# Attention in a fused ViT block: transposed probabilities and values kept whole in float32, row maxima written negated

## The reference, cut to what matters

```
h = embed(x) ; prepend cls_tok                      # [16, 37, 192]
n = layernorm(h)
Q, K = rope(n @ Wq.T), rope(n @ Wk.T) ; V = n @ Wv.T   # 12 heads of 16
s = Q K^T / sqrt(16), causal mask, softmax over keys
h = h + (softmax(s) V) @ Wo.T
h = h + moe(layernorm(h))                           # 8 experts, top 2, hidden 768, exact gelu
```

## Time and profile before

| | |
|---|---|
| median of 3 runs | 245.99 us (243.65 to 252.13) |
| the profiled execution | 244.32 us, of which the span of the trace is 242.5 us |
| VectorE busy | 153.4 us, 63% |
| TensorE busy | 182.8 us, 75% |
| GpSimd busy | 96.1 us, 40% |
| mean granted TensorE clock | 0.802 of 2.4 GHz |

### The profile page before, as it was taken

The page is one execution under the profiler, slowest core; times in us unless marked ns, Lnnn a source line. Parts: engine busy times, 40 slices in busy tenths (PEclk is TensorE's granted clock), DMA queues, the critical chain, the costliest instruction groups (busy, mean ns, idle before and its releaser), DMA issues.

```text
span 242.5 us, 3838 instructions
## 1 busy us (share of the span) xinstructions
PE 182.8 (75%) x1065; PEld 140.7 (58%) x1065; DVE 153.4 (63%) x436; ACT 104.4 (43%) x313; POOL 96.1 (40%) x77
## 2 busy tenths in 40 slices
PE   3999999659799499729829343454899999999830
PEld 2887343245666295615815122254799999999720
DVE  0133756859878968797994888996356455564410
ACT  2011333477687366527030022900656566566500
POOL 1012265739404600853925736930023233433241
PEclk9999999977587956955555555559999999999995
DMA  6945999999999400100100795202032342422211
GB/s 164 312 111 138 278 285 279 285 279 251 201 194 210 112 3 1 39 0 4 39 0 13 213 278 143 50 26 76 22 63 38 59 59 42 67 52 20 33 19 16
DMA packets 25656, 27.12 MB, mean 112 GB/s; under 512 B 4880, under 2 KB 21928, under 8 KB 25634
## 3 DMA queue, kind: packets, MB, share of 16 engines
q1 hardware_dynamic: 21378, 24.16, 40.1%
q0 software_dynamic: 4256, 2.69, 7.8%
HBM read 23.73 MB, written 8.64 MB: 133 GB/s over the span
## 4 chain that ended last, share of the span: by engine, by line
PE 50%; DVE 23%; DMA 10%; issue 8%; ACT 3%; SPq 2%; POOL 1%; ACTq 0%; POOLq 0%; DVEq 0%
PE bank L708 8%; DMA out_y<-y,tokblk 7%; PE bank L463 6%; PE bank L534 5%; PE bank L732 4%; PE bank L489 4%; DVE sneg L1091 3%; DVE ao L1118 3%; PE bank L718 3%; DVE tablei L1240 3%; PE bank L495 2%; PE bank L734 2%; PE bank L550 2%; DVE pay L1015 2%; DMA wtok_sb<-in_w_tok 1%
## 5 line engine op out<-in xcount | busy, mean ns | idle before, releaser
L446 POOL DMA_INDIRECT out_y<-y,tokblk x14 | 21.9, 1562 | 55.2 <-DVE y L1281 23.8
L372 POOL TENSOR_TENSOR rstd<-veps,nhalf 111x1 f32<-111x1 f32 (+1 forms) x12 | 7.0, 584 | 58.5 <-DVE veps L999 58.5
L732 PE MATMUL bank<-we,hthi 128*128 x84 | 25.9, 371 | 1.4 <-DVE htlo L1272 1.4
L827 ACT ACTIVATE probs<-bank,sneg 111x111 f32<-111x111 f32 (+1 forms) x72 | 18.2, 347 | 18.2 <-DVE sneg L1091 18.1
L380 POOL TENSOR_TENSOR we<-raw,we 128x1152 fp32r<-128x1152 f32 x8 | 20.9, 2617 | 4.8 <-ACT we L883 4.7
L1091 DVE TENSOR_SCALAR sneg<-smax 111x4 f32<-111x4 f32 (+1 forms) x18 | 21.0, 1166 | 0.6
L708 PE MATMUL bank<-we,xahi 128*128 x56 | 20.2, 361 | 1.4 <-DVE xb L1254 1.4
L405 POOL DMA_INDIRECT dispatched<-pay,rowu x12 | 16.5, 1373 | 11.9 <-DVE rowu L1167 10.1
L734 PE MATMUL bank<-we,htlo 128*128 x84 | 21.1, 251 | 0.0
L463 PE MATMUL bank<-wtok_sb,x_sb 128*111 128x192 f32 (+1 forms) x72 | 17.5, 403 | 4.1 <-DMA wtok_sb<-in_w_tok 4.1
L947 ACT ACTIVATE hid<-bank 128x384 f32<-128x384 f32 x28 | 13.8, 492 | 10.2 <-PE bank L708 10.2
(11 more groups left out here) (162 smaller groups left out, 491.2 us busy)
## 6 DMA issues: line engine op xcount, KB each, us to landing
dispatched<-in_pad_rows SPq DMA_DIRECT2D x1, 5350.5 KB, 37.4
raw<-in_w SPq DMA_DIRECT2D x8, 576.0 KB, 12.8
raw<-in_w_a SPq DMA_DIRECT2D x8, 384.0 KB, 8.9
raw<-in_w_bb SPq DMA_DIRECT2D x8, 384.0 KB, 9.4
xin<-dispatched SPq DMA_DIRECT2D x14, 130.5 KB, 2.1
x_sb<-in_patches SPq DMA_DIRECT2D x5, 333.0 KB, 5.8
raw<-in_w_b SPq DMA_DIRECT2D x8, 192.0 KB, 9.1
wtok_sb<-in_w_tok SPq DMA_DIRECT2D x3, 192.0 KB, 3.5
```

Of the source, the lines that this page charges most:

```text
L446: pool.indirect_dma_start(out, bass.IndirectOffsetOnAxis(ap=tokblk[:, b:b + 1], axis=0), y[:, b % 2, :], None, compute_op=ALU.add).then_in ...
L732: mm(o[:, 0:2 * D], hthi[:, f, :], w, start=(f == 0), stop=False)
L827: last = fn(probs[0:n, b, hd, 0:n], bank[g][0:n, TOK * j:TOK * j + n], ACT.Exp, bias=sneg[0:n, b, hd:hd + 1], scale=float(HD) ** -0.5)
```

## The change

The transposed probabilities are copied whole to `pt` in float32: groups 0 and 1 by ScalarE (`turned`, where `high` was), group 2 by VectorE (where `low` of group 2 was). `low` and `high` of the second part go. `vp` is float32 with 17 columns a head (16 values and the one), written by one copy on ScalarE, so lines 797, 1061 and 418 go with their semaphores. `values` makes one float32 matmul a head. The scale 1/4 of the scores is put into the rope tables (each of cosine and sine is multiplied by 1/2), and the reduction for the row maxima writes the negated maximum at once, so that line 1091 goes. `norm_out` is a reciprocal and one multiplication that reads PSUM.

```diff
-PC = 2 * HD + 1
+PC = HD + 1
-        vp = early("vp", [TOK, TILES, HEADS, VC], BF16)
+        vp = early("vp", [TOK, TILES, HEADS, PC])
-        pth = second("pth", [TOK, 2, HEADS, TOK], FP16)
-        ptl = second("ptl", [TOK, 2, HEADS, TOK], FP16)
+        pt = second("pt", [TOK, 2, HEADS, TOK])
+        def turned_copied(engine, t, g):
+            if g < 2:
+                engine.wait_ge(pt_act, 2 * t + g + 1)
+            else:
+                engine.wait_ge(pt_dve, t + 1)
@@ gpsimd, after each tile's sum of line 415
-                pool.wait_ge(v2_ready, t + 1)
-                nc.gpsimd.tensor_tensor(vp[0:n, t, :, PC:VC], vr..., vp[0:n, t, :, HD + 1:PC], ALU.subtract)
@@ tensor, probs_t
-                        pe.wait_ge(ptl_ready, i - 1)
+                        turned_copied(pe, *divmod(i - 2, GROUPS))
@@ tensor, values
-                        pe.wait_ge(ptl_ready, GROUPS * t + hd // HG + 1)
+                        turned_copied(pe, t, hd // HG)
-                    mm(... pth, vp[0:PC]) ; mm(... pth, vp[PC:VC]) ; mm(... ptl, vp[0:PC])
+                    last = mm(bank[7][0:n, c:c + PC], pt[0:n, b, hd, 0:n], vp[0:n, t, hd, :], start=True, stop=True)
@@ scalar, v_parts
-                fn(vp[0:n, t, :, HD + 1:PC], vr[0:n, b, :]..., ACT.Copy).then_inc(v2_ready, 1)
@@ scalar, exps
-                              bias=sneg[0:n, b, hd:hd + 1], scale=float(HD) ** -0.5)
+                              bias=sneg[0:n, b, hd:hd + 1])
@@ scalar, the loop
-                    high(i - 1, 0) ; high(i - 1, 1)
+                    turned(i - 1, 0) ; turned(i - 1, 1)
...
-                    high(i - 1, 2)
@@ vector, rope
-                v.tensor_tensor(vr..., bank[2 + b]..., vp[0:n, t, :, 0:HD], ALU.subtract).then_inc(vr_ready, 1)
@@ vector, scores_max
-                    step(v.tensor_reduce(smax[0:n, b, hs], s, AX.X, ALU.max))
-                    v.tensor_scalar(sneg[0:n, b, hs], smax[0:n, b, hs], -float(HD) ** -0.5, None, ALU.mult)
+                    v.tensor_reduce(sneg[0:n, b, hs], s, AX.X, ALU.max, negate=True).then_inc(max_ready, 1)
@@ vector, in place of low
+            def turned(t, g):
+                dve.wait_ge(pt_done, i + 1)
+                if t >= 2:
+                    dve.wait_ge(pv_done, t - 1)
+                v.tensor_copy(pt[0:n, b, HG * g:HG * g + HG, 0:n], bank[3 + i % 2]...).then_inc(pt_dve, 1)
@@ vector, norm_out
-                v.reciprocal(rsum[0:n, b, :], o[:, :, HD])
-                step(v.tensor_copy(a, o[:, :, 0:HD]))
-                step(v.tensor_tensor(a, o[:, :, HD + 1:PC], a, ALU.add))
-                v.tensor_tensor(a, a, rsum..., ALU.mult)
+                step(v.reciprocal(rsum[0:n, b, :], o[:, :, HD]))
+                v.tensor_tensor(a, o[:, :, 0:HD], rsum..., ALU.mult)
@@ vector, the loop
-                    low(i - 1, (0, 1))
...
-                    low(i - 1, (2,))
+                    turned(i - 1, 2)
@@ tables on the host
-        "rope_cos": np.cos(m_theta).astype(np.float32)[pos],
+        "rope_cos": np.cos(m_theta).astype(np.float32)[pos] * np.float32(HD ** -0.25),
```

More of the change, by code:

```diff
@@ L58 @@
 EARLY = 6
-VC = 3 * HD + 1
 G0, G1, LG, CT = 0, TOK, 2 * TOK, 256
-PC = 2 * HD + 1
+PC = HD + 1
 BLOCK_WARM_UP = 18
@@ L236, in vit_block @@
         qk_ready = sem("qk_ready")
-        v1_ready = sem("v1_ready")
-        vr_ready = sem("vr_ready")
-        v2_ready = sem("v2_ready")
-        v3_ready = sem("v3_ready")
+        v_ready = sem("v_ready")
         ones_ready = sem("ones_ready")
@@ L248, in vit_block @@
         pt_done = sem("pt_done")
-        pth_ready = sem("pth_ready")
-        ptl_ready = sem("ptl_ready")
+        pt_act = sem("pt_act")
+        pt_dve = sem("pt_dve")
         pv_done = sem("pv_done")
@@ L491, in project @@
                 if t >= 2:
-                    pe.wait_ge(vr_ready, t - 1)
-                    pe.wait_ge(v1_ready, t - 1)
+                    pe.wait_ge(v_ready, t - 1)
                 for j, (a, w) in enumerate(((hnta, wqkva_sb), (hntb, wqkvb_sb))):
@@ L528, in scores @@
                     elif g == 2:
-                        pe.wait_ge(vr_ready, TILES - 1)
-                        pe.wait_ge(v1_ready, TILES - 1)
+                        pe.wait_ge(v_ready, TILES - 1)
                     q, k = (qta[:, b, 0:n], kbda[:, b, HG * g:HG * g + HG, 0:n]) if g < 2 else \
@@ L556, in values @@
                 n, b = ROWS[t], t % 2
-                pe.wait_ge(v3_ready, t + 1)
+                pe.wait_ge(v_ready, t + 1)
                 if t == 0:
@@ L564, in values @@
                     if hd % HG == 0:
-                        pe.wait_ge(ptl_ready, GROUPS * t + hd // HG + 1)
+                        turned_copied(pe, t, hd // HG)
                     c = hd * PC
-                    mm(bank[7][0:n, c:c + PC], pth[0:n, b, hd, 0:n], vp[0:n, t, hd, 0:PC], start=True, stop=False)
-                    mm(bank[7][0:n, c:c + HD], pth[0:n, b, hd, 0:n], vp[0:n, t, hd, PC:VC], start=False, stop=False)
-                    last = mm(bank[7][0:n, c:c + PC], ptl[0:n, b, hd, 0:n], vp[0:n, t, hd, 0:PC],
-                              start=False, stop=True)
+                    last = mm(bank[7][0:n, c:c + PC], pt[0:n, b, hd, 0:n], vp[0:n, t, hd, :], start=True, stop=True)
                 if hd == HEADS - 1:
@@ L837, in high @@
                     act.wait_ge(pv_done, t - 1)
-                fn(pth[0:n, b, HG * g:HG * g + HG, 0:n],
+                fn(pt[0:n, b, HG * g:HG * g + HG, 0:n],
                    bank[3 + i % 2][0:n, 0:HG * TOK].rearrange("p (h s) -> p h s", s=TOK)[:, :, 0:n], ACT.Copy)\
-                    .then_inc(pth_ready, 1)
+                    .then_inc(pt_act, 1)
             def copy_attended(t):
@@ L888, in _ @@
                 if i >= 1:
-                    high(i - 1, 0)
-                    high(i - 1, 1)
+                    turned(i - 1, 0)
+                    turned(i - 1, 1)
                 if i >= 2:
@@ L1089, in scores_max, with turned @@
                     s = bank[g][0:n, 0:HG * TOK].rearrange("p (h s) -> p h s", s=TOK)[:, :, 0:n]
-                    step(v.tensor_reduce(smax[0:n, b, hs], s, AX.X, ALU.max))
-                    v.tensor_scalar(sneg[0:n, b, hs], smax[0:n, b, hs], -float(HD) ** -0.5, None, ALU.mult)\
-                        .then_inc(max_ready, 1)
-            def low(t, groups):
+                    v.tensor_reduce(sneg[0:n, b, hs], s, AX.X, ALU.max, negate=True).then_inc(max_ready, 1)
+            def turned(t, g):
                 n, b = ROWS[t], t % 2
-                for g in groups:
-                    i = GROUPS * t + g
-                    hs = slice(HG * g, HG * g + HG)
-                    dve.wait_ge(pth_ready, i + 1)
-                    if t >= 2:
-                        dve.wait_ge(pv_done, t - 1)
-                    v.tensor_tensor(ptl[0:n, b, hs, 0:n],
-                                    bank[3 + i % 2][0:n, 0:HG * TOK].rearrange("p (h s) -> p h s", s=TOK)[:, :, 0:n],
-                                    pth[0:n, b, hs, 0:n], ALU.subtract).then_inc(ptl_ready, 1)
+                i = GROUPS * t + g
+                dve.wait_ge(pt_done, i + 1)
+                if t >= 2:
+                    dve.wait_ge(pv_done, t - 1)
+                v.tensor_copy(pt[0:n, b, HG * g:HG * g + HG, 0:n],
+                              bank[3 + i % 2][0:n, 0:HG * TOK].rearrange("p (h s) -> p h s", s=TOK)[:, :, 0:n])\
+                    .then_inc(pt_dve, 1)
             def norm_out(t):
@@ L1314, in constants @@
         "tok_sel": np.stack([tok % SEQ != 0, tok % SEQ == 0]).astype(np.float32),
-        "rope_cos": np.cos(m_theta).astype(np.float32)[pos],
-        "rope_sin": (np.sin(m_theta).astype(np.float32)[pos] * sign).astype(np.float32),
+        "rope_cos": np.cos(m_theta).astype(np.float32)[pos] * np.float32(HD ** -0.25),
+        "rope_sin": (np.sin(m_theta).astype(np.float32)[pos] * sign).astype(np.float32) * np.float32(HD ** -0.25),
         "mask": np.where(allowed, 0.0, -1e30).astype(bf16),
```

26 lines of the change are left out of this document (3 added, 23 removed).

## The result

The changed kernel takes 231.01 us (median of 4 runs, 229.52 to 231.54) where the kernel before takes 244.82 (4 runs beside it, 243.4 to 252.13): a ratio of 0.940, with 0.934 to 0.946 as its interval. The forecast was 232.0. The profiled execution's span is 229.3 us against 242.5. The ratios leave out runs in which a kernel was over 1.5% above its own fastest; the medians take in every run, so a difference of medians can be larger than the ratio beside it says.

What follows compares the result with a forecast made beforehand. The attention loop was taken to be bound by VectorE's SBUF instructions waiting behind GpSimd. A 12.3 us lead at tile 5's norm_out plus 0.6 in the tail gave 12.9, so 232 us; own range 228 to 235, overall 225.5 to 240.

Steps and rivals of the forecast that it cites:

- Opening: Up to the first maximum: tile 1's keys spread at about 43.9 instead of 44.86, 1.0 us gained; negated reduction nearly free.
- Tile 0: Loop's first norm_out: at about 56.5 us, ahead by 7.2, with 0.6 taken back by ScalarE and 1.0 by the values.
- Values on TensorE: Float32 matmuls in attention: pairs 0.20 or 0.37 us apart, 2.4 or 4.4 us a tile, losing 0.5 or 1.1.
- Steps 1 to 3: Loop: about 1 us net in steps 2 and 3, step 3's hold stays; tile 2's norm_out about 79, 9 ahead.
- Step 4: Loop: hold moves to choose until 96.7; tile 3's norm_out, about 92, isn't held; ahead by 10.
- Step 5: Loop: the 6.98 us stall is covered, choose then waits 1.4 us; 2 us more gained.
- Tail: After the last norm_out's start: two instructions fewer, 0.6 us; the stall at 135.77 stays, later distances kept.
- Rival 1: Loop: stalls only move from step 3 on, gain is the opening's 7.2 + 0.6: 236.5 us; chance 0.17.
- Rival 5: Row maxima: negation takes a second pass from SBUF that GpSimd holds, most stalls stay: 243 us; chance 0.07.
- Rival 3: Scatters wait for the padding copy landing at 83.75, capping Rival 2's gain at 13.5 + 3: 228 us; chance 0.03.
- Rival 4: Values: float32 weights aren't loaded beside the matmul before, so the kernel is slower: 263 us; chance 0.04.
- Rival 2: Steps 4 and 5: TensorE gets the higher clock, 5.4 us more gained: 226.5 us; chance 0.12.

Runs made afterwards that it cites:

- experiments 3 and 4: GpSimd's subtractions in the loop left out, low parts of weights filled by DMA: 3 from the kernel before, 227.94 us; 4 from the kernel after, 222.5 us.
- experiment 1: Kernel before with only the negated maxima (reduction writes them, line 1091 goes) and the scaled tables: 241.63 us, ratio 0.990.
- experiment 2: Kernel after with the negation given back as a second instruction from SBUF: 241.51 us, ratio 0.985.
- experiment 11: Kernel before with the negated reduction and norm_out's one product from PSUM, second part of the values left out of the sum: 236.96 us, ratio 0.964.
- experiment 5: Kernel after with norm_out copying to SBUF first and multiplying there: 237.54 us, ratio 0.960.
- experiment 6: Kernel after with two VectorE subtractions reading PSUM given back at the head of each step, into a scrap tile: 236.48 us.
- experiment 10: Kernel after with norm_apply's two instructions moved behind the step's last maximum, warm-up still 18: 236.39 us.
- warm_24: Kernel after with 24 instead of 18 warm-up matmuls before the first block: 227.12 us; again, beside the kernel after on one chip, 229.79 against 230.04.
- the two reorderings: Kernel after with GpSimd's subtractions ahead of router and scatters, 233.53 us; and with norm_apply behind the last maximum, 236.39 us.

## Why the prediction was right, step by step

**What bounds the loop.** Right, and shown: GpSimd's subtractions account for 11.0 of the loop's 13.9 us (experiments 3 and 4), the holds move in part to the next SBUF instruction when one is taken away (experiment 1), and 12.2 us come back when one is put back (experiment 2). The reductions and products with PSUM input ran beside GpSimd unhindered: 553 and 356 ns means. One bound was too low: I put the longest wait at the three subtractions' 6.2 us, though the earlier trace rows have one of 6.98. That one began at 115.81, inside the scatter that precedes them (115.27 to 116.61), and scatters hold VectorE too.

**Opening.** Right: 1.0 forecast, 1.15 measured between the two profiled executions, of which 0.97 lie after the first projection. The opening of one and the same code varies by up to 2.9 us, but all of that lies ahead of the first projection. From the first projection's first matmul to the first maximum it is 20.90 or 20.91 us in all four profiled executions with the old projections (the kernel before and experiments 1, 3 and 11) and 19.93 in all ten with the new ones. The negation costs nothing: 553 ns against 555.

**Tile 0.** `norm_out` at 55.63, forecast 56.5: ahead by 8.05 for 7.2. From the first exponentials to there it is 9.77 us where I had 10.4; the 0.6 that I let ScalarE take back is as large as the difference, which doesn't show that it is it.

**Values on TensorE.** Right: 0.19 and 0.38 us a pair (2.3 and 4.5 us a tile) where the row of line 602 gave 0.20 and 0.37. The prediction's estimate by four passes of columns would have had this part cost nothing. The pace of 17 columns is that of 8, as a pace set by the load of the weights would have it. Tile 5 says so too: with 37 weight columns instead of 111 and the same 17 moving ones its records start 0.065 us apart at the lower clock, about a third of 0.188 (its weights have fewer rows as well, 37 for 111, which no run separates).

**Steps 1 to 3.** Right in place and size: line 996 held for 3.11 us, tile 2's `norm_out` at 77.84 for "about 79", of whose 1.2 us 0.9 are tile 0's.

**Step 4.** That the hold moves to `choose` is right (3.54 us on line 1112, GpSimd's end at 95.25 for 96.7). Tile 3's `norm_out` is at 90.66 for 92. Whether the old hold of the product there "wasn't last" the runs answer two ways: from tile 3's `norm_out` to tile 4's it is 17.29 us with the product held for 4.15 us (experiment 1) and 17.89 with it free (experiment 11), which speaks for the judgement, but 18.01 against 16.76 between experiment 5 and the kernel after, which puts at most 1.25 us on it.

**Step 5.** Mis-sized. Tile 4's `norm_out` was forecast some 18 us after tile 3's (92 to about 110, through by 110.4) and came 16.76 after it (90.66 to 107.42): about 1.3 of the loop's 2.6 us of error. Against the kernel before the gain grew in this step from 9.9 to 15.3 us. The part of it that I had named, the hold of 6.98 us that falls out, is what experiment 1 shows by itself: this distance is 22.17 us before and 17.29 with the negation alone, 4.9 us where I had put 2. I had GpSimd's next end 15.1 us after the one of step 4, and it was 14.3. The two subtractions saved don't explain the rest: with them back (experiment 6) the distance is 17.02 for 16.76. The wait of `choose` is there, with 0.90 us for 1.4.

**Tail.** The term itself held: -0.46 up to the first block for -0.6, and the old hold stays (line 999 at 120.11, 3.44 us for 3.44). Failed, though small, is that the blocks keep their distances: +1.9 measured in all, by 1.5 in the first block at the lower clock and 0.8 in the chain of scatter-adds. "If the tail's distances aren't kept" was named as a way to be wrong. Nor is the clock part shown to come from the change: the kernel before had no such loss in its one profiled execution, but kernels with its code in all but the loop (experiments 1, 3 and 11) had 5.3 to 5.4 us in the first block.

So two errors of opposite sign, 2.8 us too little up to the last `norm_out` and 2.5 too much in the tail, left 231.01 against 232.0. The mechanism was right, the closeness is partly luck: without the clock's 1.5 us in the first block the time would have been about 2.5 us under the forecast.

**The rivals.** Rival 1, that stalls only move from step 3 on (236.5), is refuted for the whole change, whose lead grew from 8.05 us at tile 0 to 15.06 at tile 5; it is what each part alone does, at 241.63 and 241.51. Rival 5's mechanism, a negation in a second pass, was built and gave 241.5 for its 243. Rival 3's showed up in experiment 10. Rival 4 is refuted by the values' pace. Rival 2's reason (a clock higher than before in steps 4 and 5) didn't occur: tile 3's values had the higher level before and after, and from 92 us on the clock row still has 5, with 2.42 us for half a tile of values at 102.42.

**Still open.** Why the end's scatter-adds take 0.8 us longer, and which event decides how much of the first two blocks gets the low clock. No version of the same computation that I ran beats the kernel after: warm_24 is 0.25 us apart on the same chip, within the spread, and the two reorderings are slower by 2.5 and 6.4 us in the median.

## What to carry to other kernels

Where two engines exclude each other, look at what reads only SBUF in the whole window of the other engine, not at the instruction that happens to be held: taking the negation out alone gave 4.5 us of the loop, the whole change 13.9. Giving an instruction an input in PSUM, or folding it into its predecessor, frees it even where it saves little work. Price a stall by what TensorE does behind it, and compare stretches between two events rather than whole spans when the opening varies more than the term in question.

## What the runs showed of the hardware that I had not expected

A waiting VectorE instruction is not always let in between GpSimd's: one on 37x4 elements waited 6.46 us, from inside a scatter through three subtractions back to back (experiment 2), and one of 111x64 waited 7.07 us in the same manner (experiment 10). That GpSimd's indirect DMA alone holds it is seen where no subtraction follows (0.51 us for 0.17, experiment 3). An idle time of 1.95 us on TensorE was followed by the lower granted clock (0.50 from 58 to 62 us), and `norm_out` came 4.5 us late (experiment 5, one execution). The same opening code took from 42.43 to 45.34 us in nine executions, all of the spread ahead of the first projection; one difference between them is in the second embedding tile of line 459, 4.11 us in one and 2.20 in another. And true float32 matmuls of 17 columns on 111 are two records each, 97 or 188 ns a record, the pace of those of 8 columns; with 37 weight columns it is 65 ns at the lower clock.
